# Late record scatters issued between the gathers of the first edge pass

## The chip, the core and the metric

The kernel runs on one core of a Trainium2 chip. The metric is the device time of one execution in microseconds (us); the kernel before takes 3430.24 us, the median of three runs (3429.38 to 3430.73). Besides these there is one profiled execution, from which every row below comes.

## The reference

Four graph layers run one after the other on the same graph of 3125 nodes and 50,000 edges (sorted by destination, at random sources), with 256 features. Each has a layer norm and a ReLU in front and a residual around it:

```python
edge_index = jnp.stack([src, dst])
h = jnp.maximum(_layernorm(x, axis=-1), 0.0)
x = x + _L0_gnn_ref(h, edge_index, ...)          # agg = segment_sum(h[src], dst); two dense layers with batch norm
h = jnp.maximum(_layernorm(x, axis=-1), 0.0)
x = x + _L1_gnn_ref(h, src, dst, edge_weight, edge_weight_n2, ...)
#   a_in  = segment_sum(feat_in[src] * iw, dst);  a_out = segment_sum(feat_out[dst] * ow, src);  a GRU-like gate
h = jnp.maximum(_layernorm(x, axis=-1), 0.0)
x = x + _L2_gnn_ref(h, src, dst, edge_weight, ...)   # as L0, with other weights
h = jnp.maximum(_layernorm(x, axis=-1), 0.0)
x = x + _L3_gnn_ref(h, ..., edge_index, 16)          # an edge MLP: relu([x_i, x_j - x_i] @ W1) @ W2, mean over edges
```

The graph is known only on the device. So the kernel first sorts the edges by node block, once for the destinations and once for the sources, and then runs over them in five passes.

## The kernel before

**The sort.** Edges are held as 125 partitions x 400 columns (EP, EC). For the destination order ("recs 0") the records are placed with matmuls. For the source order ("recs 1") GpSimd scatters them: one indirect DMA per column writes 125 records of 16 bytes into one of five tables in DRAM (`recs_dram`, column modulo 5, SPLIT), and the five are later loaded and added. Of the 400 columns 50 are scattered before the placing loop and 240 within it, 30 in each of its 8 turns, from small staging buffers that ScalarE fills. The last 110 (LATE) are copied by ScalarE into their own place in SBUF (`late_slot`, `late_rec`) before the loop; the semaphore `late_saved` tells of it. A scatter into table k waits until the last one into that table has landed (`sc_done[k]`), so at most five are open.

**An edge pass.** 220 units (PAIRS) of up to 256 edges in 196 groups (GROUPS) are worked off. For a group ScalarE casts two index columns into `stg_idx` (L1032, semaphore `staged`), GpSimd gathers 2 x 128 rows of 256 floats from the table of node features in DRAM into a ring of seven groups (RING_G) in SBUF (`gather_pair`, L834), SyncE passes the landings on to TensorE (`relay`, semaphore `arrived`), VectorE makes two one-hot matrices, TensorE multiplies them with the rows (L2116) and VectorE adds the product to the sums (L1497). ScalarE casts the index columns of group g + 7 when TensorE is done with the units of group g. On GpSimd a pass is a loop of 27 turns of seven groups, and then 6 groups more and one gather of 80 rows (`gathers`, L849). The pass of the sources of layer 1 (`gathers_wide`, L860) gathers rows of 512 floats, and the last stage (`gather_hidden`, L945) gathers for the edge MLP.

**Around the change.** GpSimd runs, in this order: constants, the 290 early scatters, the gathers of pass 0 (layer 0), the 110 late scatters, the gathers of pass 1, then the rest. Each engine works off its own list in order, and semaphores are all that ties them. Behind pass 0 the other engines run the dense part of layer 0: the transposes of the sums and h times (1 + eps) (z0, L2166 and L1554), the first dense layer (up0, L2156, results taken by ScalarE at L1070), batch norm, the second (down0), batch norm, the residual and the layer norm, whose result SyncE stores as the next table (L680, L682). GpSimd waits for that table (`table_ready(1)`) before the gathers of pass 1. SyncE then loads the five record tables (L699), each behind its `sc_done`, and VectorE adds them up between units of pass 1 (`merge`).

Of the kernel before, what the change touches and what calls it, by code (L numbers as in the profile page):

```python
# [24 lines left out]
GROUPS = -(-E // EDGES)  # L25
RING_G = 7
# [18 lines left out]
SC = 10  # L45
SPLIT = 5
# [11 lines left out]
HALVES = PRE_H + STB * PIT  # L58
LATE = EC - HALVES * SC
# [72 lines left out]
def gnn_kernel(nc, a, out):  # L132
# [5 lines left out]
    table = nc.dram_tensor("table", [N, D], f32).ap()  # L138
# [8 lines left out]
    with ctx:  # L147
# [3 lines left out]
        def sem(name):  # L151
            return ctx.enter_context(nc.semaphore(name))

        def sems(name, n):
            return [sem(f"{name}{k}") for k in range(n)]
# [19 lines left out]
        late_slot = acc[:, wcol0 + NB:wcol0 + NB + LATE].bitcast(i32)  # L175
        late_rec = acc[:, wcol0 + NB + LATE:wcol0 + NB + 5 * LATE].rearrange("p (c r) -> p c r", r=4)
# [4 lines left out]
        rowsbuf = rows_flat.rearrange("p (c s) -> p c s", s=S)  # L181
# [229 lines left out]
        stages_begun = sem("stages_begun")  # L411
# [14 lines left out]
        late_saved = sem("late_saved")  # L426
# [3 lines left out]
        sc_done = sems("sc_done", SPLIT)  # L430
# [331 lines left out]
        def _(pool):  # L762
# [44 lines left out]
            def scatter(col, index, rec):  # L807

                k = col % SPLIT
                pool.indirect_dma_start(  # L810
                    out=recs_dram[k], out_offset=bass.IndirectOffsetOnAxis(ap=index, axis=0), in_=rec,
                    in_offset=None).then_inc(sc_done[k], 16)
# [16 lines left out]
            def gather_pair(i, j, src, dst):  # L829

                pool.wait_ge(staged, i * RING_G + j + 1)
                pool.sem_inc(stages_begun, 1)
                for c in (2 * j, 2 * j + 1):
                    pool.indirect_dma_start(  # L834
                        out=dst[:, c, 0:D], out_offset=None, in_=src,
                        in_offset=bass.IndirectOffsetOnAxis(ap=stg_idx[:, c:c + 1], axis=0)
                    ).then_inc(landed[j], 16)

            def gathers(n, src, dst):

                with pool.Fori(n * GITS, (n + 1) * GITS - 1) as i:
                    for j in range(RING_G):
                        gather_pair(i, j, src, dst)
                for j in range(RING_G - 1):
                    gather_pair((n + 1) * GITS - 1, j, src, dst)
                pool.wait_ge(staged, (n + 1) * GITS * RING_G)
                pool.sem_inc(stages_begun, 1)
                c = 2 * RING_G - 2
                pool.indirect_dma_start(  # L849
                    out=dst[0:END_ROWS, c, 0:D], out_offset=None, in_=src,  # L850
                    in_offset=bass.IndirectOffsetOnAxis(ap=stg_idx[0:END_ROWS, c:c + 1], axis=0)
                ).then_inc(landed[RING_G - 1], 16)
# [20 lines left out]
            def table_ready(layer):  # L873
                pool.wait_ge(tab_written, 16 * (NB // GROUP + 1) * (layer + 1))
# [12 lines left out]
                    scatter_half((i, h // STB + 1, h), h % STB)  # L887
            pool.wait_ge(order_ready, 2)
            table_ready(0)
            gathers(0, table, rowsbuf)  # L890

            pool.wait_ge(late_saved, 1)
            pool.sem_inc(stages_begun, 1)
            for k in range(LATE):
                col = HALVES * SC + k
                pool.wait_ge(sc_done[col % SPLIT], 16 * (col // SPLIT))
                pool.sem_inc(stages_begun, 1)
                scatter(col, late_slot[:, k:k + 1], late_rec[:, k, :])

            table_ready(1)  # L900
            gathers(1, table, rowsbuf)
            pool.wait_ge(gates_kept, UNITS + 1)
            for k in range(GST):
# [16 lines left out]
            nc.gpsimd.memset(agg_flat[0][:, FULL_T * TB * S:NB * S], 0.0).then_inc(sums_clear, 1)  # L920
            pool.wait_ge(tab_written, 16 * (2 * (NB // GROUP + 1) + -(-NB // STORE2)))
            gathers(3, table, rowsbuf)

            all_filled("T3")
# [1561 lines left out]
```

## Time and profile before

| | |
|---|---|
| Median of three runs | 3430.24 us (3429.38 to 3430.73) |
| Span of the profiled execution | 4205.1 us |
| Busy: TensorE (PE), its weight loads (PEld) | 2930.9 us (70%), 1849.8 us |
| VectorE (DVE), ScalarE (ACT), GpSimd (POOL) | 2117.9, 1141.1, 2373.5 us |
| Indirect DMAs issued by GpSimd | 2404: 1173 narrow gathers, 391 wide, 440 in the last stage, 400 scatters |
| Idle time of GpSimd before the gathers of L834 | 767.8 us |
| Bytes over HBM | 403.39 MB read, 34.24 MB written, 104 GB/s |

The span is that of the profiled execution, from its first to its last instruction. Its time by the clock of the timed runs is not recorded; the span alone is 775 us above the median of the runs. A row of an instruction gives start and duration, the line of the kernel, what is written and read, and in brackets how long its engine had been idle and who ended that. "issue" is idle time in which the engine waited for nothing that the profile shows, and "remote" a wait whose end the profile can't lay at anybody's door. The busy time of an indirect DMA on GpSimd is its issuing, not its transfer. Rows of waits read: total us, how often, the longest.

### The profile page before, as it was taken

The page shows a single profiled execution, that of the slowest core. Times are in us where ns is not written, and L with a number is a line of the kernel's source. Part 1 is how long each engine was busy: PE and PEld are TensorE (multiplying, and loading weights), DVE is VectorE, ACT ScalarE, POOL GpSimd, SP SyncE. Part 2 cuts the span into 40 slices and gives each one's busy share as a digit, 9 for nine tenths or more (in the row PEclk, how much of TensorE's full clock was granted, in tenths as well). Part 3 has the DMA queues.
Part 4 walks back from the last instruction along what each step waited for, and adds up shares of the span by engine and source line. Part 5 has one row for each costly group of instructions (what it writes and reads, how often), then busy time and mean ns, then how long its engine had stood idle before and what let it go on. Part 6 is the DMA issues. An engine that isn't in the chain of part 4 may idle for free. (4 is left out here: it accounts for less than half of the span.)

```text
span 4205.1 us, 55362 instructions
## 1 busy us (share of the span) xinstructions
PE 2930.9 (70%) x11580; PEld 1849.8 (44%) x11581; DVE 2117.9 (50%) x6459; ACT 1141.1 (27%) x3023; POOL 2373.5 (56%) x2458
## 2 busy tenths in 40 slices
PE   3677776555542846677588887755554899988989
PEld 1233333333321434444333332433333548888878
DVE  6566664333320455444456655533333576667664
ACT  1466661000000330000000000300000356666662
POOL 3544445666667046666666666666666226666662
PEclk6788887667665867888799999976676999999999
DMA  3000002333320043333366666433333136666664
GB/s 123 2 1 1 1 1 74 90 89 90 90 56 2 20 139 88 101 106 105 109 176 180 177 176 178 138 89 89 87 91 86 34 124 186 187 188 185 189 187 143
DMA packets 184321, 438.94 MB, mean 104 GB/s; under 512 B 53924, under 2 KB 78623, under 8 KB 184233
## 3 DMA queue, kind: packets, MB, share of 16 engines
q0 software_dynamic: 135568, 372.32, 31.3%
q1 hardware_dynamic: 48665, 65.55, 4.7%
q8 instruction: 42, 0.69, 0.1%
q14 instruction: 46, 0.38, 0.0%
HBM read 403.39 MB, written 34.24 MB: 104 GB/s over the span
## 5 line engine op out<-in xcount | busy, mean ns | idle before, releaser
L834 POOL DMA_INDIRECT acc<-table,stg_idx x1170 | 1128.5, 965 | 767.8 <-issue 349.1
L2116 PE MATMUL psum<-acc,oh 128*128 x2600 | 871.4, 489 | 637.7 <-issue 456.5
L2116 PEld LDWEIGHTS psum<-acc,oh 128*128 128x128 f32 x2600 | 598.2, 244 | 912.3 <-issue 821.2
L1497 DVE TENSOR_TENSOR acc<-acc,psum 128x257 f32 (+1 forms) x660 | 276.0, 418 | 962.7 <-remote 565.4
L1032 ACT CAST stg_idx<-rec 128x2 int32 (+1 forms) x784 | 148.4, 193 | 2113.0 <-remote 841.2
L945 POOL DMA_INDIRECT TT<-qtable,stg_row x440 | 424.1, 964 | 282.4 <-PE psum L2428 150.9
L860 POOL DMA_INDIRECT H<-gtable,stg_idx x391 | 379.1, 970 | 199.5 <-issue 116.5
L2205 PE MATMUL psum<-H 125*128 125x440 bf16 x1600 | 375.5, 399 | 154.2 <-issue 48.2
L2137 PE MATMUL psum<-H,oh 128*128 x880 | 426.2, 630 | 79.8 <-issue 31.1
L810 POOL DMA_INDIRECT recs<-acc,sst_idx x290 | 284.6, 981 | 338.1 <-ACT acc L977 255.6
L2428 PE MATMUL psum<-oh,TT 128*128 128x128 f32 x3520 | 444.3, 277 | 34.7 <-issue 26.0
L2428 PEld LDWEIGHTS psum<-oh,TT 128*128 128x128 f32 x3520 | 427.8, 192 | 69.5 <-issue 32.3
L1488 DVE TENSOR_SCALAR oh<-iota,stg_lw 128x128 f32<-128x128 f32 x1320 | 404.0, 357 | 97.6 <-issue 94.1
L2205 PEld LDWEIGHTS psum<-H 125*128 125x128 f16 (+1 forms) x1600 | 165.9, 107 | 364.1 <-issue 122.4
L1921 DVE TENSOR_TENSOR TT<-TT,psum 128x1024 f32<-128x1024 f32 x220 | 267.4, 1216 | 98.8 <-PE psum L2416 40.3
L2137 PEld LDWEIGHTS psum<-H,oh 128*128 128x128 f32 x880 | 166.6, 198 | 329.9 <-issue 329.4
L1247 ACT ACTIVATE TT<-TT 128x1024 f32<-128x1024 f32 x220 | 232.8, 1058 | 247.7 <-issue 121.1
L2416 PE MATMUL psum<-PT,ohT 128*128 x880 | 260.7, 415 | 30.3 <-issue 15.8
L1928 DVE TENSOR_TENSOR H<-H,psum 128x512 f32 x220 | 149.9, 681 | 114.7 <-remote 58.5
L1603 DVE TENSOR_SCALAR H<-H 125x128 bf16<-125x128 f16 x400 | 103.3, 258 | 185.0 <-PE psum L2205 82.4
L1505 DVE TENSOR_TENSOR H<-H,psum 128x256 f32 x220 | 91.5, 416 | 182.7 <-remote 76.9
L2416 PEld LDWEIGHTS psum<-PT,ohT 128*128 128x128 f32 x880 | 149.7, 189 | 60.5 <-issue 42.9
(277 smaller groups left out, 3210.7 us busy)
## 6 DMA issues: line engine op xcount, KB each, us to landing
acc<-table,stg_idx POOLq DMA_INDIRECT x1173
TT<-loc_dram SPq DMA_DIRECT2D x22, 320.0 KB
TT<-qtable,stg_row POOLq DMA_INDIRECT x440
Wm<-loc_dram SPq DMA_DIRECT2D x22, 320.0 KB
H<-gtable,stg_idx POOLq DMA_INDIRECT x391
gtable<-H SPq DMA_DIRECT2D x24, 256.0 KB
qtable<-H SPq DMA_DIRECT2D x24, 256.0 KB, 2.2
table<-H SPq DMA_DIRECT2D x8, 640.0 KB
```

What stands on the lines that cost most here:

```text
L810: pool.indirect_dma_start(out=recs_dram[k], out_offset=bass.IndirectOffsetOnAxis(ap=index, axis=0), in_=rec, in_offset=None).then_inc(sc_d ...
L834: pool.indirect_dma_start(out=dst[:, c, 0:D], out_offset=None, in_=src, in_offset=bass.IndirectOffsetOnAxis(ap=stg_idx[:, c:c + 1], axis=0 ...
L860: pool.indirect_dma_start(out=ring_rows[0:r, c, :], out_offset=None, in_=gtable, in_offset=bass.IndirectOffsetOnAxis(ap=stg_idx[0:r, c:c + ...
L945: pool.indirect_dma_start(out=hbuf[:, c, :], out_offset=None, in_=qtable, in_offset=bass.IndirectOffsetOnAxis(ap=stg_row[:, q * CH_IT + c: ...
L1488: last = V.tensor_scalar(oh[:, c, :], iota1[:, :], stg_lw[:, c, 0:1], stg_lw[:, c, wcol:wcol + 1], ALU.is_equal, ALU.mult)
L1497: V.tensor_tensor(at, at, sum_bank(j)[:, 0:w], ALU.add).then_inc(added, 1)
L1921: V.tensor_tensor(t, t, spread_banks(g), ALU.add).then_inc(joined, 1)
L2116: last = mm(sum_bank(j)[:, 0:w], oh[:, 2 * j + k, :], rows_flat[:, ds(start[j] + k * S, w)], start=(k == 0), stop=(k == 1))
L2137: last = mm(sum_bank(j)[:, 0:w], oh[:, 2 * j + h, :], rows_in[:, ds(start[j] + h * step, w)], start=(h == 0), stop=(h == 1))
L2205: last = mm(ps[k][:, 0:CHUNKS], ring[:, c, :], hi_ring[:, c, :], start=False, stop=False)
L2416: last = mm(dst[:, k, :], ohT[:, 2 * j + k, :], PTf[:, ds(block0 * (2 * HID // P) + part * HID, HID)], start=(part == 0), stop=(part == 1))
L2428: last = mm(hidden_bank(g)[:, k * P:(k + 1) * P], hbuf[:, c, k * P:(k + 1) * P], oh[:, c, :], start=(c == 2 * j), stop=(c == 2 * j + 1))
```

## The change

The 110 late scatters leave the place behind pass 0. The gathers of pass 0 are written out group by group instead of in a loop, and behind group g stand those late scatters k with g x 110 / 196 <= k < (g + 1) x 110 / 196, rounded down: none or one per group. The wait for `late_saved` stands ahead of the first gather. The tail of `gathers`, the gather of 80 rows, becomes a function of its own. Passes 1 and 3 keep their loop. Nothing is changed on the other engines.

```diff
+            def late_scatter(k):
+
+                col = HALVES * SC + k
+                pool.wait_ge(sc_done[col % SPLIT], 16 * (col // SPLIT))
+                pool.sem_inc(stages_begun, 1)
+                scatter(col, late_slot[:, k:k + 1], late_rec[:, k, :])
+
+            def gathers_scattering():
+
+                pool.wait_ge(late_saved, 1)
+                pool.sem_inc(stages_begun, 1)
+                for g in range(GROUPS):
+                    i, j = g // RING_G, g % RING_G
+                    if g < GROUPS - 1:
+                        gather_pair(i, j, table, rowsbuf)
+                    for k in range(g * LATE // GROUPS, (g + 1) * LATE // GROUPS):
+                        late_scatter(k)
+                gather_end(0, table, rowsbuf)
+
...
             table_ready(0)
-            gathers(0, table, rowsbuf)
-
-            pool.wait_ge(late_saved, 1)
-            pool.sem_inc(stages_begun, 1)
-            for k in range(LATE):
-                col = HALVES * SC + k
-                pool.wait_ge(sc_done[col % SPLIT], 16 * (col // SPLIT))
-                pool.sem_inc(stages_begun, 1)
-                scatter(col, late_slot[:, k:k + 1], late_rec[:, k, :])
+            gathers_scattering()
 
             table_ready(1)
             gathers(1, table, rowsbuf)
```

On GpSimd (POOL), at the start of pass 0, stands before, as the head of the loop (`acc` holds the ring of gathered rows, `stg_idx` the index columns):

```order
L841 UNCONDITIONAL_BRANCH [waits tab_written,order_ready]
L841 ISA
L834 DMA acc<-table,stg_idx 128x256 [waits staged]
L834 DMA acc<-table,stg_idx 128x256
L831 REGISTER_ALU
L834 DMA acc<-table,stg_idx 128x256 [waits staged]
L834 DMA acc<-table,stg_idx 128x256
```

and now, with the first two scatters into `recs` behind the second and the fourth group:

```order
L834 DMA acc<-table,stg_idx 128x256 [waits late_saved,order_ready,tab_written,staged]
L834 DMA acc<-table,stg_idx 128x256
L834 DMA acc<-table,stg_idx 128x256 [waits staged]
L834 DMA acc<-table,stg_idx 128x256
L810 DMA recs<-acc 56323x4 [waits sc_done0]
L834 DMA acc<-table,stg_idx 128x256 [waits staged]
L834 DMA acc<-table,stg_idx 128x256
L834 DMA acc<-table,stg_idx 128x256 [waits staged]
L834 DMA acc<-table,stg_idx 128x256
L810 DMA recs<-acc 56323x4 [waits sc_done1]
```

The loop is gone, and about every second group is followed by a scatter.

At the end of pass 0 GpSimd has before (the last gather of the pass is that of 80 rows, and 110 scatters follow it up to the branch into the loop of pass 1):

```order
L834 DMA acc<-table,stg_idx 128x256 [waits staged]
L834 DMA acc<-table,stg_idx 128x256
L849 DMA acc<-table,stg_idx 80x256 [waits staged]
L810 DMA recs<-acc 56323x4 [waits late_saved,sc_done0]
L810 DMA recs<-acc 56323x4 [waits sc_done1]
L810 DMA recs<-acc 56323x4 [waits sc_done2]
```

and now:

```order
L834 DMA acc<-table,stg_idx 128x256 [waits staged]
L834 DMA acc<-table,stg_idx 128x256
L810 DMA recs<-acc 56323x4 [waits sc_done3]
L810 DMA recs<-acc 56323x4 [waits sc_done4]
L872 DMA acc<-table,stg_idx 80x256 [waits staged]
L860 UNCONDITIONAL_BRANCH [waits tab_written]
```

The scatters are all ahead of the last gather, and the wait for the next table (tab_written) follows it at once.

## Rows read from the trace of the kernel before

**Rows 1.** Busy time of the engines by stage, granted clock, DMA share.

```profile
core 0: us, PE busy (x) PEld busy (x) DVE busy (x) ACT busy (x) POOL busy (x), PEclk, DMA share, GB/s
39.00:650.00 611.00, 406.75 (x1703) 181.80 (x1703) 378.32 (x1613) 348.92 (x1134) 284.74 (x291) 0.77 0.04 8
650.00:1222.50 572.50, 326.15 (x902) 212.97 (x903) 189.84 (x712) 39.55 (x196) 375.71 (x391) 0.70 0.31 89
1222.50:1499.00 276.50, 138.34 (x447) 75.26 (x446) 73.58 (x189) 66.50 (x117) 106.70 (x110) 0.72 0.09 26
1499.00:2086.50 587.50, 382.28 (x1166) 248.76 (x1166) 269.72 (x869) 47.86 (x206) 378.34 (x391) 0.78 0.35 104
2086.50:2714.00 627.50, 518.85 (x1218) 227.23 (x1219) 365.14 (x1132) 74.06 (x278) 407.35 (x410) 0.94 0.60 172
2714.00:3290.00 576.00, 302.79 (x902) 206.67 (x900) 212.36 (x706) 38.66 (x194) 375.35 (x390) 0.70 0.31 89
...
3500.00:4205.00 705.00, 637.08 (x4362) 569.46 (x4361) 467.85 (x859) 413.46 (x698) 394.08 (x410) 1.00 0.62 181
```

**Rows 2.** Timeline of GpSimd (POOL) within the first pass.

```profile
689.67 0.95 POOL L834 DMA_INDIRECT acc<-table,stg_idx  x1 [0.30 <-issue]
694.15 0.95 POOL L834 DMA_INDIRECT acc<-table,stg_idx  x1 [3.53 <-ACT stg_idx L1032]
```

**Rows 3.** Waits of GpSimd in the four passes and the last stage, in order.

```profile
POOL acc L834 <- issue: 125.9, 350, 3.2
POOL acc L834 <- ACT stg_idx L1032: 88.6, 40, 18.2
...
POOL acc L834 <- issue: 109.5, 340, 2.0
POOL acc L834 <- ACT stg_idx L1032: 99.3, 49, 4.5
...
POOL H L860 <- issue: 116.5, 352, 2.7
POOL H L860 <- ACT stg_idx L1032: 82.9, 39, 3.9
...
POOL acc L834 <- issue: 113.8, 346, 2.2
POOL acc L834 <- ACT stg_idx L1032: 86.0, 43, 4.2
...
POOL TT L945 <- PE psum L2428: 143.1, 82, 2.3
POOL TT L945 <- issue: 98.9, 322, 0.6
```

**Rows 4.** The late scatters as a group of their line.

```profile
L810 POOL DMA_INDIRECT recs<-acc x110: 964/971/1019, 1222.6 to 1361.5; - x110
```

**Rows 5.** Waits of GpSimd between 1223 and 1500 us.

```profile
POOL acc L834 <- DMA table<-H: 136.6, 1, 136.6
POOL recs L810 <- issue: 33.2, 109, 0.3
```

**Rows 6.** Timeline of VectorE and of ScalarE beside the late scatters, and after.

```profile
1283.48 0.75 DVE L1554 SCALAR_TENSOR_TENSOR acc<-TT,vec,psum 128x512 f32<-128x512 f32 x1 [10.45 <-issue]
1294.68 0.75 DVE L1554 SCALAR_TENSOR_TENSOR acc<-TT,vec,psum 128x512 f32<-128x512 f32 x1 [10.45 <-remote]
...
1305.94 0.69 ACT L1070 ACTIVATE H<-psum,vec 128x512 f32<-128x512 f32 x1 [92.90 <-remote]
...
1377.97 2.42 ACT L1070 ACTIVATE H<-psum,vec 128x512 f32<-128x512 f32 x4 [4.91 <-remote]
```

**Rows 7.** DMA queues from 1223 to 1362 us.

```profile
q0 software_dynamic: 3536, 0.31, 3.0%
```

**Rows 8.** ScalarE's copy that ends with late_saved.

```profile
L1101 ACT COPY acc<-TT x1: 552/552/552, 108.5 to 108.5; 125x440 f32<-125x440 f32 x1
```

**Rows 9.** SyncE's loads of the record tables.

```profile
L699 SPq DMA_DIRECT2D rec<-recs x1: 892/892/892, 1493.0 to 1493.0; - x1
```

More of the change, by code:

```diff
@@ L845, in gathers, with gather_end @@
                     gather_pair((n + 1) * GITS - 1, j, src, dst)
+                gather_end(n, src, dst)
+            def gather_end(n, src, dst):
                 pool.wait_ge(staged, (n + 1) * GITS * RING_G)
```

## The prediction

> **What bounds the kernel now.** I first cut the span into its stages [rows 1]. Columns to compare are the length of a stage, what each engine was busy in it, and the granted clock. The sort is 39 to 650 us; the four edge passes are 650 to 1222.5, 1499 to 2086.5, about 2087 to 2666 (the wide gathers, inside the fifth line) and 2714 to 3290; the last stage follows at 3500. In the first pass GpSimd was busy 375.7 of 572.5 us, TensorE 326.2, VectorE 189.8, ScalarE 39.6. GpSimd's busy time leaves out the gap before each issue. Its timeline shows that gap: 0.30 us before almost every gather, so one gather takes 0.96 + 0.30 = 1.26 us [rows 2, 3]. The pass has 391 of them: 391 x 1.26 = 493 us of 572.5. The DMA engines are 31% busy meanwhile [rows 1], so what is full is the issuing engine. GpSimd sets the pace of this pass, and the others follow.
>
> The remaining 79 us are waits inside the pass. GpSimd waited 88.6 us for index columns from ScalarE, of which 18.2 are the wait before the pass, and 125.9 us for "issue" [rows 3]. Taking off the ordinary gap, 390 x 0.30 = 117 us, 88.6 - 18.2 + 125.9 - 117 = 79 us are left. The same sum gives 92 us in the second pass, 82 in the wide one, 83 in the fourth and, with 410 gaps, 143.1 + 98.9 - 123 = 119 us of waiting for TensorE in the last stage [rows 3].
>
> Then comes the stage that the change empties: 1222.5 to 1499. On GpSimd the 110 late scatters stand there back to back, first start 1222.6, last 1361.5 [rows 4], 109 times with 0.3 us before them (33.2 us in all) [rows 5], hence a step of (1361.5 - 1222.6) / 109 = 1.275 us and 110 x 1.275 = 140 us. After them GpSimd is idle 136.6 us until the node table has landed [rows 5]. Seen from GpSimd alone the scatters lie in free time.
>
> The other engines tell more. While the scatters are issued, VectorE and ScalarE together start one instruction every 11.2 us (VectorE's 1283.48 and 1294.68, then ScalarE's 1305.94), each with nothing else to do; after the last scatter, from 1377.97 on, ScalarE does four such instructions in 2.42 us [rows 6]. TensorE is busy only 138.3 of 276.5 us in the whole stage [rows 1]. So the others go on only once per 9 or so scatters (11.2 / 1.275). From 1378 to 1499 it is 121 us at full pace; what was done in the 155 us before that I estimate at 29 us, from the single durations of 0.69 and 0.75 us [rows 6] with TensorE's part between them. The stage's own length is then 150 us, and 127 us are stall.
>
> **Span against median.** The profiled span is 4205.1 us, the timed median 3430.24: 775 us of the span do not exist in the timed runs, 18%. That decides this case, because the stalls are what the change could win. What can shrink by 775 us? The waits beside GpSimd's issuing: 79 + 92 + 82 + 83 us in the four passes, 127 in the stage of the late scatters, 119 in the last stage: 582 us. The step of a gather: at most its gap, 0.30 x 1564 gathers of the four passes = 469 us. Were all stalls real in a timed run, the step could give 469 at most and 306 us would have to come from the sort and the dense stages, where I see no reason. Were none real, 193 are left, for the sort's own waits and a step shorter by about 4% (1.22 us per scatter). The second closes far more easily. So I read most of the stall as belonging to the profiled execution. This is an inference from the sums, not something the trace shows.
>
> **The change, part by part.**
> (a) Added to the first pass: 110 scatters on the engine that sets its pace. In the span 110 x 1.275 = 140 us [rows 4, 5]; at the timed step 110 x 1.22 = 134 us. What can hide them is only GpSimd's waiting in that pass: 79 us in the profile, and, by the paragraph above, 0 to 20 in a timed run; I take 10. Bounds: +55 (134 - 79) to +140; taken: +124, near the upper end, since the stretches of unbroken gathers [rows 2] are the rule in this pass. The scatters go to the same queue as the gathers, but their data are small: 110 of them kept the 16 DMA engines 3.0% busy [rows 7]. The ring is seven groups deep, 14 gathers of 1.26 us, far above the few us of a landing. No other engine comes near: with 493 + 140 us of steps it is 633 us for GpSimd against TensorE's 326.
> (b) Each scatter waits for the one five before it (sc_done). Between two on one counter there will now be some nine gathers and four scatters, over 15 us; in the old place five steps, 6.4 us, were enough for all but one of 110 [rows 5]. Cost nothing. Behind such a wait stand only gathers.
> (c) The wait for late_saved moves ahead of the first gather. ScalarE wrote that data at 108.5 us [rows 8], the pass begins at 650. Nothing.
> (d) The loop of the first pass is written out: 390 gathers, 110 scatters. The 110 scatters before the change were also written out, and had 0.30 us before each [rows 5]; the loop's 350 "issue" waits hold 125.9 - 105 = 21 us above 0.30 a piece, which bounds what its turns cost [rows 3]. Bounds -21 to +21; taken 0.
> (e) Taken from behind the pass: the 110 scatters. GpSimd's next work waits for the table, which the dense stage sets. Gain between 0 (no stall in a timed run) and 127 us (all of it). 140 us of scatters are just covered by a stage of 150, so leaving them out gives nothing by itself. Taken: 4.
> (f) SyncE's loads of the five record tables stand behind the table stores on its queue and start at 1493.0 [rows 9], long after the last scatter; earlier scatters move nothing there. The merges on VectorE follow from these.
> Sum: 124 - 4 = +120 us on 3430: **3550 us**.
> For the profiled execution the same parts give +61 to +140 for (a) and -127 for (e): a span of 4139 to 4218, almost the old one. The profile of the changed kernel may look neutral while the timed runs are slower.
>
> **The rivals.**
> A. All of the stall is real in a timed run. For it: it is in every stage where GpSimd issues unbroken [rows 3, 6]. Against it: the 775 us. Then (e) is -127 and (a) is +55 if the scatters fill the waits, +134 if each stop of the ring stays as it is: 3430 - 72 to 3430 + 7, middle 3397. With a share f of the stall real and the waits filled, the balance is 134 - 79 f - 127 f, so the change wins from f = 0.65 up. Chance 0.18, faster but for its upper edge.
> B. About half of it is real: (e) -64, (a) 134 - 40 = +94: 3460. Slower, since f is under 0.65. Chance 0.14.
> C. The scatters cost no time in the pass, because issuing hides behind the transfers, and gain nothing behind it: 3430. For it: GpSimd's waits of 79 us in the profile. Against it: the 1.26 us steps against DMA engines busy 31%. Chance 0.06. The Trainium skill ("DMA: Bandwidth & Descriptors", Issuing engines are not separate DMA queues) says that the time on the sequencer to initiate a DMA is usually small relative to the DMA itself; by that rule this rival would be the likeliest. In this trace the issue takes 1.275 us for each scatter and the transfers of 110 of them 3.0% of the DMA engines [rows 5, 7], so here the rule does not hold.
> D. The forecast: the stalls are nearly all of the profiled execution, GpSimd bounds the pass: 3520 to 3575. Chance 0.62.
>
> **How the numbers follow.** The likeliest is D, 3550. Its upper end is 3430 + 140 and a little; the range goes down over B to the upper part of A, 3415, and leaves out A's lower part (0.14) and a few hundredths above. About 0.2%, 7 us, is what a measurement of this kernel can tell from no change. Slower: D and most of B, 0.73. Same: C, 0.07 with the edges of A. Faster: A and a little of B, 0.20.
>
> **What would show it.** In the profile after: the first pass longer by 61 to 140 us, with 4 scatters in every 14 gathers at 1.27 us each; the stage behind it near 150 us with TensorE busy most of it and no 11 us steps; passes two to four unchanged. If the timed median rises by 100 us or more while the span stays, D is right. If the median falls, the stall was real. If the first pass does not grow in the timed runs, GpSimd was not what bounds it, and (a) is wrong.

## The result

In the first comparison the changed kernel takes 3577.43 us (median of four, 3575.95 to 3578.44) and the kernel before 3429.81 (four, 3429.01 to 3430.73): ratio 1.0428, 95% interval 1.0416 to 1.044. It is slower by 147.6 us, where +120 was forecast; 3577.4 lies 2.4 us above the range.

One thing must be known for all numbers below. In the first comparison and in one more the kernel before took 3427 to 3430 us; in four others, each on another chip, the same kernel took 4212 to 4266 us. I call the first condition A and the second B. The profile of before that stands ahead of the prediction (span 4205.1 us) shows condition B. No chip is on record with two comparisons, so the runs can't tell whether the condition belongs to the chip or to the time. Times of kernels are set against each other only within one comparison.

The changed kernel's profile is in condition A: its span is 3575.3 us. The first row below is its sort, then the first pass, the dense stage, the second pass (columns: the stretch, its length, busy time of each engine with instructions, granted clock, DMA share, GB/s).

```profile
39.00:431.00 392.00, 343.73 (x1703) 158.56 (x1702) 364.79 (x1611) 338.10 (x1131) 300.85 (x290) 0.93 0.07 13
431.00:1070.00 639.00, 391.35 (x910) 240.56 (x910) 212.97 (x715) 39.75 (x196) 486.63 (x501) 0.62 0.28 81
1070.00:1211.30 141.30, 120.32 (x438) 68.65 (x438) 71.96 (x186) 66.85 (x117) 0.03 (x1) 0.93 0.15 49
1211.30:1708.80 497.50, 373.01 (x1167) 237.06 (x1167) 277.26 (x874) 47.88 (x207) 375.92 (x391) 0.86 0.41 123
```

Against [rows 1] every stage but the first pass is shorter: the sort 392 us instead of 611, the dense stage 141 instead of 276.5, the second pass 497.5 instead of 587.5. That difference is not the change's, since the next section shows nearly the same lengths for the kernel before in condition A. The first pass of the changed kernel, on GpSimd:

```profile
1060.14 1.01 POOL L810 DMA_INDIRECT recs<-acc  x1 [0.30 <-issue]
1061.45 0.97 POOL L834 DMA_INDIRECT acc<-table,stg_idx  x1 [0.30 <-issue]
1062.73 0.95 POOL L834 DMA_INDIRECT acc<-table,stg_idx  x1 [0.30 <-issue]
1063.98 0.95 POOL L834 DMA_INDIRECT acc<-table,stg_idx  x1 [0.30 <-issue]
```

GpSimd's waits in that pass (total, times, longest):

```profile
POOL acc L834 <- issue: 115.5, 379, 0.3
POOL recs L810 <- issue: 33.5, 110, 0.3
POOL acc L834 <- ACT stg_idx L1047: 3.8, 11, 0.7
```

No wait is longer than 0.7 us, where [rows 3] had single waits of up to 3.2 and 18.2. GpSimd issues from the first gather to the last without a break. A scatter between gathers takes 1.01 + 0.30 = 1.31 us, and the gather behind it 0.97 instead of 0.95.

### The profile page after: what moved, and what is told of

It is laid out like the page before. It is cut to its first block and busy times, and to the rows that moved or that the text cites. A ratio compares the mean times of both kernels' runs of the same rounds, so it can differ in the third digit from the quotient of the medians.

```text
span 3575.3 us, 55118 instructions
## 1 busy us (share of the span) xinstructions
PE 2868.7 (80%) x11580; PEld 1829.2 (51%) x11581; DVE 2162.1 (60%) x6459; ACT 1133.1 (32%) x3023; POOL 2385.9 (67%) x2458
## 5 line engine op out<-in xcount | busy, mean ns | idle before, releaser
L2131 PE MATMUL psum<-acc,oh 128*128 x2600 | 970.6, 524 | 528.6 <-issue 139.7
L2131 PEld LDWEIGHTS psum<-acc,oh 128*128 128x128 f32 x2600 | 626.7, 259 | 870.0 <-issue 769.7
L2152 PE MATMUL psum<-H,oh 128*128 x880 | 406.5, 603 | 43.5 <-SPq L649 31.1
L2443 PE MATMUL psum<-oh,TT 128*128 128x128 f32 x3520 | 428.2, 275 | 0.2
L810 POOL DMA_INDIRECT recs<-acc,sst_idx x290 | 300.9, 1038 | 120.6 <-issue 85.9
L2220 PE MATMUL psum<-H 125*128 125x440 bf16 x1600 | 314.6, 350 | 14.5 <-ACT H L1000 13.3
L2152 PEld LDWEIGHTS psum<-H,oh 128*128 128x128 f32 x880 | 158.2, 189 | 282.8 <-issue 281.9
L2220 PEld LDWEIGHTS psum<-H 125*128 125x128 f16 (+1 forms) x1600 | 142.0, 98 | 187.5 <-issue 77.2
L1000 ACT ACTIVATE H<-H 125x128 f16<-125x128 bf16 x400 | 154.4, 386 | 0.0
```

Of the source, the lines that this page charges most:

```text
L810: pool.indirect_dma_start(out=recs_dram[k], out_offset=bass.IndirectOffsetOnAxis(ap=index, axis=0), in_=rec, in_offset=None).then_inc(sc_d ...
L2131: last = mm(sum_bank(j)[:, 0:w], oh[:, 2 * j + k, :], rows_flat[:, ds(start[j] + k * S, w)], start=(k == 0), stop=(k == 1))
L2152: last = mm(sum_bank(j)[:, 0:w], oh[:, 2 * j + h, :], rows_in[:, ds(start[j] + h * step, w)], start=(h == 0), stop=(h == 1))
L2220: last = mm(ps[k][:, 0:CHUNKS], ring[:, c, :], hi_ring[:, c, :], start=False, stop=False)
L2443: last = mm(hidden_bank(g)[:, k * P:(k + 1) * P], hbuf[:, c, k * P:(k + 1) * P], oh[:, c, :], start=(c == 2 * j), stop=(c == 2 * j + 1))
```

## The experiments

**The kernel before again, none of its late scatters, the pass written out, and half of the scatters moved.** These four ran together, in condition A, beside 19 runs of the kernel before (median 3427.46 us).

The kernel before, unchanged, for a profile:

> The kernel before, unchanged, for a second profile of it beside the first, whose span of 4205.1 us was 775 us above the timed median. If the long span belongs to that one execution, this span is near 3428 us, as the changed kernel's span of 3575.3 us is near its median; the first pass then takes 391 x 1.26 = 493 us, and GpSimd waits for the next table, behind the late scatters, only what the stage of 141 us leaves over 110 x 1.275 = 140 us, so a few us. If profiling itself stretches the kernel before, the span is again about 4200 us with the 11.2 us steps.

Measured: 3428.82 us, span 3427.1. So profiling does not stretch the kernel. Its stages, in the order of the rows of after (sort, first pass, dense stage with the scatters, second pass):

```profile
39.00:431.00 392.00, 343.75 (x1703) 158.93 (x1703) 364.57 (x1611) 338.12 (x1131) 300.48 (x290) 0.93 0.07 13
431.00:923.50 492.50, 323.63 (x904) 211.95 (x903) 202.21 (x713) 39.95 (x196) 373.24 (x391) 0.76 0.36 104
923.50:1066.50 143.00, 122.52 (x448) 70.38 (x446) 74.55 (x192) 68.12 (x117) 106.44 (x111) 0.92 0.15 41
1066.50:1561.30 494.80, 367.94 (x1167) 234.94 (x1168) 275.61 (x872) 46.78 (x207) 374.39 (x391) 0.87 0.43 126
```

From the start of its first gather (431.2) to the end of its last (923.3) the pass is 492.1 us for 391 gathers, 1.26 each, with nothing over. The dense stage is 143 us although 110 scatters stand beside it: TensorE's busy 122.5 us there is about what it is with none beside it (120.3 in the rows of after). On GpSimd that stage ends so:

```profile
1063.55 0.97 POOL L810 DMA_INDIRECT recs<-acc  x1 [0.30 <-issue]
1065.19 0.97 POOL L810 DMA_INDIRECT recs<-acc  x1 [0.67 <-issue]
1066.46 0.98 POOL L834 DMA_INDIRECT acc<-table,stg_idx  x1 [0.30 <-issue]
```

The last scatter is followed by the first gather of the second pass after the ordinary gap. The scatters fill the dense stage to its end; by the next run, where it is 141.8 us without them, they reach about 1 us beyond it.

No late scatters (their places in the record tables stay empty; SyncE's wait is set to the 290 others):

```diff
-            pool.wait_ge(late_saved, 1)
-            pool.sem_inc(stages_begun, 1)
-            for k in range(LATE):
...
-                scatter(col, late_slot[:, k:k + 1], late_rec[:, k, :])
```

> The kernel before with the 110 late scatters left out altogether (the record tables of the source order stay incomplete). My theory, GpSimd's issuing behind the first pass is covered by the dense stage: no gain, 3425 to 3430 us. Rival A, a real stall of the other engines beside unbroken issuing: faster by the share of 127 us that is real; at half of it 3366 us.

Measured: 3429.70 us, ratio 1.0005 (0.9996 to 1.0015). In condition A the 110 scatters behind the pass are free. GpSimd has this wait in their place:

```profile
POOL acc L834 <- DMA table<-H: 149.6, 2, 141.8
```

The pass written out, all scatters behind it:

```diff
-                    for k in range(g * LATE // GROUPS, (g + 1) * LATE // GROUPS):
-                        late_scatter(k)
...
             gathers_scattering()
+            for k in range(LATE):
+                late_scatter(k)
```

> The first pass written out as in the changed kernel, but all 110 scatters behind it, as before. Theory that the price is the issuing alone: 3430 us, within 5. Rival, writing out the pass (a longer instruction stream on GpSimd) costs part of the 148 us: at a fifth of it 3460 us.

Measured: 3427.92 us, ratio 1.0001 (0.9991 to 1.0011). The written-out pass costs nothing that was measured; the 147.6 us comes from where the scatters stand.

Half of them in the pass (55 spread, 55 behind):

```diff
-                    for k in range(g * LATE // GROUPS, (g + 1) * LATE // GROUPS):
+                    for k in range(g * (LATE // 2) // GROUPS, (g + 1) * (LATE // 2) // GROUPS):
...
+            for k in range(LATE // 2, LATE):
+                late_scatter(k)
```

> 55 late scatters between the gathers of the first pass, 55 behind it. Theory, each scatter in the pass costs its step of 1.31 us and each behind it nothing: 3430 + 55 x 1.34 = 3504 us, half of the 147.6 us. Rival, the pass has some slack that the first scatters fill: under 3495 us. Rival, scatters behind cost too when there are fewer: over 3510 us.

Measured: 3497.82 us, ratio 1.0208 (1.0191 to 1.0225), +70.4 us. The pass and the dense stage of it:

```profile
431.50:996.60 565.10, 366.70 (x909) 232.38 (x908) 206.97 (x714) 39.70 (x196) 429.48 (x446) 0.67 0.32 91
996.60:1136.40 139.80, 118.56 (x442) 66.03 (x441) 73.03 (x189) 66.96 (x117) 53.24 (x57) 0.95 0.16 50
```

The pass grows by (565.1 - 492.1) / 55 = 1.33 us for each scatter, with 110 by (639.0 - 492.1) / 110 = 1.335. The price is linear; there is no slack for the first ones to fill. The dense stage is 139.8 us, 3 less than with all 110 behind it, which accounts for 70 in place of 73.

**The changed kernel in condition B.**

> The changed kernel, unchanged, beside the same kernel before as the next three. The last comparison had the kernel before at 4211.8 us, and the long steps of the profile of before in timed runs too. If the kernel before takes about 3430 us here, this takes 3575 to 3578. If it takes about 4210, the stall is real in both: the scatters add 110 x 1.33 = 146 us to the pass and empty a stage of 276 us down to 143: 4210 + 13, between 4200 and 4240 us.

Measured: 4287.42 us against 4266.36, ratio 1.0038 (1.0018 to 1.0059), +21 us, where +13 was expected (between -10 and +30 by the limits given; the kernel before took 56 us more than assumed). The first pass and dense stage of the changed kernel, and the first pass as in the kernel before on the same chip (from the run with 165 scatters behind it, below, whose first pass is the kernel before's):

```profile
668.00:1401.00 733.00, 380.44 (x901) 230.51 (x902) 191.08 (x710) 40.12 (x198) 487.70 (x501) 0.61 0.25 70
1401.00:1544.00 143.00, 123.61 (x448) 70.44 (x446) 74.29 (x193) 66.85 (x117) 0.00 (x1) 0.92 0.15 48
668.80:1253.50 584.70, 313.02 (x904) 211.12 (x901) 187.79 (x702) 39.73 (x196) 374.68 (x391) 0.72 0.30 87
```

The emptied stage takes 143 us instead of the 276.5 of [rows 1], as long as in condition A: its stall of 133 us is real in timed runs of condition B, and is there only beside the scatters. From the start of its first gather (668.4) to the end of its last (1400.6) the pass is 732.2 us; the same gathers and scatters take 639.0 us in condition A, so 93 us of waits are in it, and 584.7 - 492.1 = 93 us are in the pass without the scatters. The scatters fill none of them: in condition B too they lengthen the pass by 147.5 us, 1.34 for each.

**All scatters in one row inside the pass** (no scatter between the other gathers):

```diff
-                    for k in range(g * LATE // GROUPS, (g + 1) * LATE // GROUPS):
+                    for k in range(LATE if g == GROUPS // 2 else 0):
                         late_scatter(k)
```

It was meant to tell in condition A what the change between gathers and scatters costs. All four comparisons fell in condition B:

> All 110 late scatters in one row in the middle of the written-out first pass, behind group 98, none between the other gathers. Theory, the price is GpSimd's issuing and the changed kernel pays 1.335 us per scatter because each stands between gathers (1.01 us against 0.97 in a row, and a longer gather behind it): here 110 x 1.275 = 140 us of pass, and 2 us less in the dense stage, so 3565 us against 3575 for the changed kernel. Rival, spreading is free and the position alone does not matter: 3575. Rival, a clump starves the other engines for 140 us and they need time to catch up: over 3580.

> All 110 late scatters in one row in the middle of the written-out first pass. Where the kernel before takes about 3430 us: 3565 us by the theory that a scatter between gathers costs 1.335 and one in a row 1.275, 3575 if it makes no difference, over 3580 if the others have to catch up. Where it takes about 4210: 4230, as before.

> All 110 late scatters in one row in the middle of the written-out first pass. Where the kernel before takes about 3430 us: 3565 us if a scatter between gathers costs 1.335 and one in a row 1.275, 3575 if that makes no difference, over 3580 if the others have to catch up. Where it takes about 4210 to 4270: 19 to 26 us above it, as twice before.

> All 110 late scatters in one row in the middle of the written-out first pass. Where the kernel before takes about 3430 us: 3565 us if a scatter between gathers costs 1.335 and one in a row 1.275, 3575 if that makes no difference, over 3580 if the others have to catch up. Where it takes over 4200: 19 to 26 us above it, as three times before.

Measured: 4230.55 against 4211.83 (1.0042), 4292.08 against 4266.36 (1.0051), 4287.90 against 4265.60 (1.0049), 4282.99 against 4265.87 (1.0046; intervals from 1.0024 to 1.0069). The second of them ran beside the changed kernel, 4287.42: in condition B the spreading makes no difference that was measured. Where 19 to 26 us above the kernel before were expected, the third lies at 22 and the fourth at 17. In condition A it was not tried; that a scatter in a row would cost 1.275 instead of 1.335 there stays open.

**Computing in the scatters' places.** 110 memsets in the pass, which issue no DMA, and all late scatters behind the pass. Each memset waits for the one before it by a semaphore of its own (`padded`):

```diff
-                        late_scatter(k)
+                        if k:
+                            pool.wait_ge(padded, k)
+                        pool.sem_inc(stages_begun, 1)
+                        nc.gpsimd.memset(pad, 0.0).then_inc(padded, 1)
...
+            for k in range(LATE):
+                late_scatter(k)
```

> In the places of the 110 scatters in the first pass stand GpSimd memsets of 128 x 1200 float32, which move nothing by DMA (110, each some 1.3 us, estimated from one of 128 x 1024 that took 1.096 us); the 110 late scatters stand behind the pass, as before. Theory, GpSimd's own time is the price: the pass grows by 110 times the memset's step as its trace shows it, 140 to 155 us, so 3565 to 3585 us. Rival, the price comes from the transfers on the shared DMA queue or their writes beside the gathers: well under, at none of it 3430 us.

> 110 memsets of 128 x 1200 float32 in the places of the scatters, the late scatters behind the pass. Their step was 1.117 us (122.8 us of 110, hardly any gap). Where the kernel before takes about 3430 us: the pass grows by about 110 x 1.12 = 123 us and by some us of waits behind them, so 3550 us; at none of it, were the price in the transfers, 3430. Where it takes about 4210: 4226, as before.

> 110 memsets of 128 x 1200 float32 in the places of the scatters, the late scatters behind the pass. Where the kernel before takes about 3430 us: 110 x 1.12 = 123 us more, with a few us of waits behind them, so 3550 us; near 3430 if the price of a scatter were in its transfer. Where it takes about 4210 to 4270: 7 to 15 us above it.

> 110 memsets of 128 x 1200 float32 in the places of the scatters, the late scatters behind the pass. Where the kernel before takes about 3430 us: 110 x 1.12 = 123 us more and a few us of waits, so 3550 us; near 3430 if the price of a scatter were in its transfer. Where it takes over 4200: 3 to 15 us above it.

All four in condition B: 4226.38 (1.0032, 1.002 to 1.0044), 4273.66 (1.0015, 1.0003 to 1.0027), 4268.19 (1.0004, 0.9989 to 1.002), 4265.57 us (1.0007, 0.9987 to 1.0026). The last two lie below what was expected (7 to 15 and 3 to 15 us above the kernel before; measured 3 and 0). So 110 memsets of 1.12 us, 123 us of work, cost 0 to 15 us. The pass of the second, and GpSimd's waits in it:

```profile
662.80:1263.90 601.10, 379.43 (x917) 235.19 (x915) 244.63 (x715) 39.84 (x196) 496.51 (x501) 0.64 0.30 85
```

```profile
POOL acc L836 <- issue: 84.1, 277, 0.3
POOL acc L836 <- ACT stg_idx L1055: 19.2, 10, 16.8
POOL acc L836 <- POOL H L860: 17.0, 103, 0.2
```

and a piece of the third's timeline:

```profile
904.66 0.96 POOL L836 DMA_INDIRECT acc<-table,stg_idx  x1 [0.30 <-issue]
905.62 1.12 POOL L860 MEMSET H<- 128x1200 f32 x1
906.90 0.96 POOL L836 DMA_INDIRECT acc<-table,stg_idx  x1 [0.17 <-POOL H L860]
```

A memset adds 1.12 + 0.17 - 0.30 = 0.99 us, since it takes the place of a gap. 492.1 + 110 x 0.99 = 601.0 us, and the pass is 601.1 us: it runs at GpSimd's full pace, and the waits of 79 to 93 us that the first pass has in [rows 3] and in the two kernels above in condition B are gone (the 16.8 us is the one ahead of the first gather). Two things follow. In a pass that GpSimd fills, its own time is the price, transfer or not: that speaks for my step (a). And with a break of 1.1 us in the issuing behind every three or four DMAs the other engines keep up in condition B. What a break does there is not shown; these kernels differ from the others also in the wait on `padded`.

**More scatters behind the pass.** 165 instead of 110, the first 55 late columns a second time:

```diff
-            for k in range(LATE):
-                col = HALVES * SC + k
+            for m in range(LATE + 55):
+                k = m % LATE
...
```

The counts that GpSimd and SyncE wait for in `sc_done` are raised to match.

> The kernel before with 165 scatters behind the first pass: the first 55 late columns are scattered a second time, same data to the same places. Theory, the dense stage of 141 us covers no more than about 110 of them, so each one more costs its whole step: 3427.5 + 55 x 1.275 = 3498 us. Rival, GpSimd has room behind the pass beyond the table (pass 1 starts later but catches up): under 3480. Rival, scatters beside the dense stage also slow its engines: over 3510.

> The kernel before with 165 scatters behind the first pass, the first 55 late columns scattered a second time. Where the kernel before takes about 3430 us: 3427.5 + 55 x 1.275 = 3498 us if the dense stage of 141 us covers about 110 and no more; under 3480 if there is room left. Where it takes about 4210: 4276, as before.

> 165 scatters behind the first pass, the first 55 late columns scattered a second time. Where the kernel before takes about 3430 us: 3498 us if the dense stage of 141 us covers about 110 and no more, under 3480 if there is room left. Where it takes about 4210 to 4270: 64 to 74 us above it.

All in condition B: +64 us (1.0159, 1.0128 to 1.0189), +74 (1.0167, 1.014 to 1.0194), +68 (1.0167, 1.0126 to 1.0208), 1.17 to 1.35 us for each of the 55. On GpSimd, in the second of them, the wait for the next table behind the scatters:

```profile
POOL acc L834 <- DMA table<-H: 136.3, 1, 136.3
```

It is 136.3 us behind 165 scatters and 136.6 behind 110 [rows 5]: in condition B the dense stage hardly moves on while scatters are issued in a row, so it can't cover them. The expectation for A was not put to the test; what shows there that the cover ends at 110 is only the timeline of the kernel before, above.

**Pauses behind the pass.** The kernel before, with GpSimd waiting for the landing of every second, or of every fourth scatter:

```diff
                 scatter(col, late_slot[:, k:k + 1], late_rec[:, k, :])
+                if k % 2:
+                    pool.wait_ge(sc_done[col % SPLIT], 16 * (col // SPLIT + 1))
+                    pool.sem_inc(stages_begun, 1)
```

> The kernel before, but behind the first pass GpSimd waits after every second late scatter until that scatter has landed, a pause of some 1.1 us (landing takes 2.1 to 2.8 us from the issue): 55 pauses, together 60 to 100 us. Where the kernel before takes about 3430 us, this exposes them: 3490 to 3530 us. Where it takes about 4210 to 4270: if what holds the other engines back is unbroken issuing, each pause lets their updates through, the dense stage runs on in the pauses and the stage of 276 us becomes shorter or stays, in spite of 60 to 100 us more on GpSimd; if the updates come at a fixed 11.2 us as long as there are scatters, the stage grows by at least half of the pauses, 30 us or more.

> The kernel before with a pause of 2.0 us behind every fourth late scatter instead of every second: 27 pauses, 27 x 1.7 = 46 us more on GpSimd behind the first pass than before. Where the kernel before takes over 4200 us: with a pause behind every second the stage was 252 us, all of it GpSimd's; if 27 pauses still let the others through, GpSimd's 187 us set the stage, and it is faster by up to 90 us than before; if four scatters in a row already hold the others back, no faster than with every second, 40 us. Where it takes about 3430: 3427 + 187 - 143 = 3472 us.

In condition B: 4224.93 against 4265.60, ratio 0.9909 (0.9875 to 0.9943), and 4187.34 against 4265.87, ratio 0.9816 (0.978 to 0.9852). Both are faster than the kernel before, by 41 and 79 us, though GpSimd does more waiting. The dense stage with 55 pauses, and in the second kernel with 27:

```profile
1236.10:1488.00 251.90, 125.31 (x452) 70.94 (x451) 84.14 (x223) 78.37 (x132) 106.74 (x110) 0.74 0.11 34
```

```profile
1249.80:1445.60 195.80, 126.72 (x451) 72.18 (x450) 85.18 (x226) 78.37 (x132) 106.48 (x110) 0.81 0.14 42
```

and GpSimd in the second:

```profile
1303.12 0.96 POOL L810 DMA_INDIRECT recs<-acc  x1 [0.30 <-issue]
1306.10 0.96 POOL L810 DMA_INDIRECT recs<-acc  x1 [2.01 <-DMA recs<-acc]
1307.37 0.97 POOL L810 DMA_INDIRECT recs<-acc  x1 [0.30 <-issue]
1308.64 0.97 POOL L810 DMA_INDIRECT recs<-acc  x1 [0.30 <-issue]
1309.91 0.97 POOL L810 DMA_INDIRECT recs<-acc  x1 [0.30 <-issue]
```

A pause adds mostly 2.01 - 0.30 = 1.7 us, which makes 140 + 27 x 1.7 = 186 us on GpSimd; with some longer ones, up to 6.9 us, it is 195 us, and the stage is 195.8 us instead of 276.5. With four scatters in a row and a pause, GpSimd is the last one again. Beside the scatters in the profile of before VectorE ran 10 instructions and ScalarE 4, in condition A 192 and 117 (the row of the kernel before there), with 27 pauses 226 and 132:

```profile
1223.00:1362.50 139.50, 32.48 (x75) 16.02 (x73) 5.90 (x10) 2.75 (x4) 106.30 (x110) 0.60 0.03 2
```

TensorE's last work of the stage, with 27 pauses and, below it, in the kernel before in condition A:

```profile
1403.17 2.19 PE L2070 MATMUL psum<-ident,H 128*128 128x128 f32 x18 [2.36 <-issue]
1059.38 2.19 PE L2067 MATMUL psum<-ident,H 128*128 128x128 f32 x18 [0.97 <-ACT TT L1019]
```

It ends 155.6 us behind the pass, against 138.3 in condition A: of the stall of 133 us about 17 are left. This version is faster than the kernel before in condition B by 1.8%, while the changed kernel was 0.4% slower. In condition A it was not run; an estimate by the sums above is 186 - 143 = 43 to 195 - 143 = 52 us more there.

## Why the prediction was right and wrong

**The direction and the mechanism held, in condition A.** Forecast D said that the stalls are not in the timed runs, that GpSimd bounds the first pass, and that leaving the dense stage gives about nothing. The pass grew by 146.9 us, the dense stage shrank from 143.0 to 141.3 us, GpSimd's waits in the pass were ordinary gaps. The second pass is 2.7 us longer (497.5 against 494.8 us), which no run explains. That both kernels were timed in A and not in B was nothing that the prediction knew of; in B the same change gives +0.4%.

**The term that was mis-sized is (a).** It said 110 x 1.22 = 134 us less 10 us of cover, 124. Measured: 110 x 1.335 = 147 us and no cover. Of the 23 us between them 10 are the cover, 6 the step of 1.22 in place of 1.275, and 7 the place between gathers. The cover failed because GpSimd's pass in condition A has no waits to fill, and in B those that it has are not filled. The step 1.22 came from the 775 us between span and median: whatever the stalls did not explain I gave to a shorter step. But the steps are the same in both conditions, 1.26 for a gather. The row for a scatter was there, 1.275 [rows 4, 5]; with it and without cover (a) is 140 us, and 3566 us the forecast. What 140 still lacks is that a scatter after a gather takes 1.01 us, not 0.967, and the gather after it 0.97, not 0.95: 110 x 0.06 = 7 us. The row of the first late scatter, the only one behind a gather, would have hinted at it: [rows 4] has a longest of 1019 ns beside a median of 971. The upper bound of (a), 140, stood as the end of the range and was too low by these 7 us.

**The split of the 775 us was half right, its reading wrong.** The waits that I took to vanish did: between [rows 1] and the kernel before in condition A the four passes lose 80, 93, 84 and 83 us and the dense stage 133, for 79, 92, 82, 83 and 127. From the last stage 119 us were to vanish, and its gathers lose 84 (696 us from the first to the last in the profile of before, 611 in condition A). The rest, 193 us, I put to "the sort's own waits and a step shorter by 4%". It was the sort alone, 611 against 392 us, 219 less; in it GpSimd waited 255.6 us for ScalarE in condition B,

```profile
POOL recs L810 <- ACT acc L977: 255.6, 25, 30.6
```

against 30.2 us, a single wait, in condition A (the kernel before again, the same view of its sort):

```profile
POOL recs L810 <- ACT acc L977: 30.2, 1, 30.2
```

And I laid the stalls to the profiled execution. They belong to the chip, or to its state at the time: in condition B timed runs take 4212 to 4266 us, and their profiles show the same stages. My marker "the span stays while the median rises" cannot be read, since the two spans were of different conditions.

**(b), (c), (d), (f)** cost nothing, as forecast: the pass with the scatters behind it written out measures 1.0001, and of the 110 scatters in the pass none waited for `sc_done`. **(e)** was taken as 4 us and is 2, by the length of the stage; leaving all scatters out measures no gain. The stage's own length, estimated at 150 us, is 143.

**The rivals.** A, the stall all real, is what condition B is: there its upper case holds, in which each stop of the ring stays as it is, with +7 us by my sum and +21 measured, slower and not faster. With the measured terms it is 147.5 for the pass less 133 for the stage, about +15. The pass did not give up its waits to the scatters (93 us of them left in 732). The decision point of 0.65 rested on that filling and falls with it. B, half of the stall, did not occur: in the profiles on record it is there in full or not at all. C, issue hidden behind transfers, is excluded in both conditions: the pass grew by 1.33 us per scatter in A and by 1.34 in B. The Trainium skill ("DMA: Bandwidth & Descriptors", Issuing engines are not separate DMA queues) has the time to initiate a DMA as usually small beside the DMA itself; in this kernel the rows disagree, with 0.97 to 1.01 us of issuing and a gap of 0.30 for each scatter, against 2.1 us (median) from its issue to its landing.

**What stays open.** What brings about condition B, and by what mechanism the steps are late there. A clock that is slower throughout is not it: the emptied dense stage takes 143 us in B and 141 in A, at granted clocks of 0.92 and 0.93. The rows say only that the other engines' steps come late while GpSimd issues in a row, and that a break of 1.1 us (memset) or 1.7 us (pause) behind three or four DMAs is enough. The change in a row against spread, the memsets and the pauses were not measured in condition A.

## What to carry to other kernels

Where an engine issues without a break from the start of a pass to its end, everything added to its list costs its full step, taken from the row of the same operation and not from a sum made to close elsewhere; in this kernel 0.06 us came on top for each scatter put between gathers. An idle stretch of the issuing engine is worth what fits into it: here 141 us, just 110 scatters. And where a profile's span is far from the timed median, get a second profile before reading the gap: it may show another condition, in which the same change is worth something else (+4.3% and +0.4% here).

## What the runs showed of the hardware

The same kernel takes 3427 to 3430 us in two comparisons and 4212 to 4266 us in four others, each on another chip, with nearly equal durations of single DMA issues (0.96 us) in both. In the slower condition the other engines stall beside unbroken issuing on GpSimd, by 133 us in a stage of 143, and 27 pauses, most of 2.0 us, made the kernel 1.8% faster. A memset of 1.12 us between two indirect DMAs adds 0.99 us on GpSimd: no gap stands ahead of it, and 0.17 us in place of 0.30 behind it. An indirect scatter takes 1.01 us to issue behind a gather and 0.97 behind another scatter.
